# x transposed by VectorE in 32x32 squares instead of by TensorE, in a MoE feed-forward kernel

## The reference

```python
q_emb = relu(q @ W3 + b3)                           # cond: [128, 512]
v_sum = sum(v, axis=1, keepdims=True)               # over the 64 tokens of a sequence
h = relu(((n * v + v_sum) * q_emb[:, None, :]) @ W2 + b2)      # n = 64
scores = softmax(h @ gate_w.T)                      # 64 experts
topk_w, topk_i = top_k(scores, 6)
# first come, first served: each expert keeps 64 of the tokens that chose it
y = sum over kept choices of topk_w * (silu(h @ w_gate[e]) * (h @ w_up[e])) @ w_down[e]   # 512 -> 352 -> 512
shared = (silu(h @ sw_gate) * (h @ sw_up)) @ sw_down                                      # 512 -> 704 -> 512
out = x + y + shared
```

## Time and profile before

| | |
|---|---|
| median of 3 runs | 1278.72 us (1278.03 to 1279.66) |
| the profiled execution | 1280.25 us, of which the span of the profile is 1278.4 us |
| PE (TensorE) busy | 1254.0 us, 98% |
| DVE (VectorE) busy | 708.5 us, 55% |
| ACT (ScalarE) busy | 338.0 us, 26% |
| granted TensorE clock, mean | 0.995 of 2.4 GHz |
| one round of the first phase, 262.23 to 338.06 us | VectorE 62.3 us busy, ScalarE 26.5 |
| from 638.70 us, the second phase | VectorE 189 of 640 us busy, DMA engines 82% |

### The profile page before, as it was taken

How to read it: one execution, slowest core, us unless ns; L and a number is a source line. 1 busy time by engine, 2 the same in 40 slices (tenths; PEclk the granted TensorE clock), 3 DMA queues, 4 the chain that set the end, 5 groups by cost and what they waited for, 6 DMA issues and landing times.

```text
span 1278.4 us, 16131 instructions
## 1 busy us (share of the span) xinstructions
PE 1254.0 (98%) x6152; PEld 934.8 (73%) x6152; DVE 708.5 (55%) x1536; ACT 338.0 (26%) x550; POOL 144.1 (11%) x118
## 2 busy tenths in 40 slices
PE   5899999999999999999999999999999999999998
PEld 5687888888888888888867666666666666666666
DVE  6688888978888787886823233232232323323322
ACT  3444332332334333233212111121111201211110
POOL 0000000000000000000001222121222222212220
PEclk8899999999999999999999999999999999999999
DMA  7814417053441615325757989969979989898952
GB/s 199 254 38 134 138 48 220 9 177 91 128 144 38 194 41 182 91 86 132 280 196 278 284 266 294 318 236 283 326 220 330 308 246 291 283 300 267 294 127 77
DMA packets 129277, 250.92 MB, mean 196 GB/s; under 512 B 21296, under 2 KB 59312, under 8 KB 127024
## 3 DMA queue, kind: packets, MB, share of 16 engines
q1 hardware_dynamic: 117712, 224.71, 52.1%
q0 software_dynamic: 11488, 25.17, 9.8%
HBM read 197.14 MB, written 61.10 MB: 202 GB/s over the span
## 4 chain that ended last, share of the span: by engine, by line
PE 92%; DVE 3%; SPq 3%; DMA 1%; ACT 1%; issue 1%; ACTq 0%; DVEq 0%
PE bank L1213 22%; PE bank L1215 21%; PE bank L1214 21%; PE bank L1446 12%; PE bank L1469 7%; SPq L459 2%; PE bank L1230 2%; PE bank L1428 1%; PE bank L1336 1%; PE bank L1335 1%; PE bank L1271 1%; PE bank L1274 1%; PE bank L1455 1%; DMA hT<-h 1%; PE bank L1284 0%
## 5 line engine op out<-in xcount | busy, mean ns | idle before, releaser
L1213 PE MATMUL bank<-hh,gu 128*128 128x512 f32 x704 | 281.3, 400 | 0.1
L1215 PE MATMUL bank<-hh,gu 128*128 128x512 f32 x704 | 274.7, 390 | 0.0
L1214 PE MATMUL bank<-hl,gu 128*128 128x512 f32 x704 | 274.3, 390 | 0.0
L1213 PEld LDWEIGHTS bank<-hh,gu 128*128 128x128 f32 x704 | 132.5, 188 | 38.7 <-issue 12.8
L863 DVE TENSOR_TENSOR prod<-bank,prod 128x512 f32<-128x512 f32 x96 | 66.1, 689 | 165.8 <-PE bank L1215 144.0
L1215 PEld LDWEIGHTS bank<-hh,gu 128*128 128x128 f32 x704 | 132.1, 188 | 28.6
L1214 PEld LDWEIGHTS bank<-hl,gu 128*128 128x128 f32 x704 | 132.4, 188 | 25.3
L616 ACT ACTIVATE ah<-prod 128x512 fp32r<-128x512 f32 x96 | 60.6, 632 | 260.8 <-DVE prod L863 260.8
L1213 PE MATMUL bank<-sdh,ah 128*128 128x512 f32 x320 | 126.8, 396 | 0.0
L1214 PE MATMUL bank<-sdl,ah 128*128 128x512 f32 x320 | 124.6, 390 | 0.0
L1215 PE MATMUL bank<-sdh,al 128*128 128x512 f32 x320 | 124.6, 389 | 0.0
(11 more groups left out here) (117 smaller groups left out, 1604.9 us busy)
## 6 DMA issues: line engine op xcount, KB each, us to landing
wg<-in_L_ffn_w_gate_dram SPq DMA_DIRECT2D x64, 704.0 KB
wu<-in_L_ffn_w_up_dram SPq DMA_DIRECT2D x64, 704.0 KB
wd<-in_L_ffn_w_down_dram SPq DMA_DIRECT2D x64, 512.0 KB
table<-hrow SPq DMA_DIRECT2D x64, 256.0 KB, 4.3
x<-in_x_dram SPq DMA_DIRECT2D x15, 1024.0 KB, 8.4
wd<-in_L_ffn_w_down_dram SPq DMA_DIRECT2D x64, 192.0 KB
out_dram<-outst SPq DMA_DIRECT2D x36, 256.0 KB, 2.7
hT<-h SPq DMA_DIRECT2D x8, 1024.0 KB, 3.9
```

What stands on the lines that cost most here:

```text
L1213: nc.tensor.matmul(o, st_h, mv_h, start=first_mm, stop=False)
L1214: nc.tensor.matmul(o, st_h, mv_l, start=False, stop=False)
L1215: return nc.tensor.matmul(o, st_l, mv_h, start=False, stop=last_mm)
```

## The change

- TensorE no longer transposes x. SyncE loads x with 32 tokens by 128 features to a block, four DMAs a chunk (eight for chunk 0, in two halves), in pieces of 512 bytes. VectorE transposes each half chunk in 32x32 squares in place (`x_turn`), sums over 32 tokens (`x_sum`), adds the sums of two neighbouring blocks (`x_pair`), computes 64 x plus the sum (`x_shift`) and multiplies by q (`x_scale`), all in `x32` itself, 1024 elements a partition at a time. `split_xm` also goes by half chunks. Since features now stand on the partitions in another order, W2, W3, b3 and the gate weights are loaded or permuted to match; q is stored twice, once for each block of a sequence (`qb`).
- PSUM banks 3 and 4, free of x, go to the condition tiles.
- Chunk 1's condition tiles are made in halves, as chunk 0's, with `logits_raw(0)` between the halves; this is ahead of body 0 now. The order of loads changes: biases before x, no wait of SyncE for `hT` of chunk 0, which ScalarE's queue now stores, in quarters, right behind each tile.
- Routing: the low part of the logits is copied by ScalarE (`take_low`), the four sums of exponentials come with ScalarE's exponentials, and ScalarE copies the transposed ranks (`take_ranks`).
- VectorE's order in a body is new, with the two halves of a `merge` separated and laid between other work.

The diff, cut to its core:

```diff
-        xm = keep("xm", [P, 2, CH])
...
+        w3p = keep("w3p", [P, QC, D])
+        qb = keep("qb", [P, 2 * B, KC])
...
+        x32 = keep("x32", [P, 2, NB, P])
...
-            return bank[(5, 6, 1, 5)[oc] if n == 0 else 5 + oc % 2]
+            return bank[(5, 6, 1, 2)[oc] if n == 0 else (3, 4, 5, 6)[oc] if n == 1 else (4, 5, 6, 4)[oc]]
...
-                    sp.wait_ge(s.xt_filled, J * (n - 1))
-                if n == 0:
-                    for j in range(J):
-                        sp.dma_start(x32[:, 0, j, :], xf[j * P:(j + 1) * P, :]).then_inc(x_begun[j], 16)
-                else:
-                    sp.dma_start(x32[:, n % 2, :, :], xf[n * CH:(n + 1) * CH, :].rearrange(
-                        "(j p) d -> p j d", p=P)).then_inc(x_loaded[n % 2], 16)
+                    sp.wait_ge(s.xml_ready, 2 * (n - 1))
+                for half in ((0, 1) if n == 0 else (None,)):
+                    b = slice(0, NB) if half is None else slice(half * (NB // 2), (half + 1) * (NB // 2))
+                    rows = xf[n * CH + b.start * SQ:n * CH + b.stop * SQ, :].rearrange("(b i) d -> i b d", i=SQ)
+                    for q in range(P // SQ):
+                        sp.dma_start(x32[q * SQ:(q + 1) * SQ, n % 2, b, :], rows[:, :, q * P:(q + 1) * P]).then_inc(
+                            x_loaded[n % 2] if half is None else x_begun[half], 16)
...
             def store_hT(u):
-                sp.wait_ge(s.cond_taken, KC * (2 * u + 1))
-                sp.dma_start(hT[u], h32[:, :, :].rearrange("p k t -> p (k t)")).then_inc(s.hT_stored, 16)
+                for k in range(KC):
+                    sp.wait_ge(s.cond_taken, KC * 2 * u + k + 1)
+                    sp.dma_start(hT[u][:, k * CH:(k + 1) * CH], h32[:, k, :]).then_inc(hT_stored[k], 16)
...
+            with nc.allow_non_contiguous_dma(reason="two vectors of 512 elements, once"):
+                sp.dma_start(conds[:, :], cond).then_inc(s.cond_loaded, 16)
+                sp.dma_start(w3s[:, :, :], W3.rearrange("(k p) o -> p k o", p=P)).then_inc(s.w3_loaded, 16)
+                for q in range(P // SQ):
+                    for b, c in ((b3, b3c), (b2, b2c)):
+                        sp.dma_start(c[q * SQ:(q + 1) * SQ, :],
+                                     b[q * P:(q + 1) * P].rearrange("(k j) -> j k", j=SQ)).then_inc(s.bias_loaded, 16)
             load_x(0)
...
             load_x(2)
-            store_hT(0)
...
+            def take_low(n):
+                act.wait_ge(s.logits_filled, n + 1)
+                wait(act, s.z_ready, n)
+                parts = logits_bank(n)[:, :].rearrange("p (j h e) -> p h j e", j=J, h=2)
+                copy(lg[:, :, :], parts[:, 1, :, :]).then_inc(s.llow_ready, 1)
+            def take_ranks(i):
+                act.wait_ge(s.ranksT_filled, i + 1)
+                wait(act, s.merge_step, MERGE_STEPS * i)
+                copy(cand[:, CAP:CAP + CH], bank[7][:, :]).then_inc(s.cand_ready, 1)
...
-                nc.scalar.activation(ez[:, :, :], z[:, :, :], ACT.Exp).then_inc(s.exp_ready, 1)
+                for j in range(J):
+                    op = nc.scalar.activation(ez[:, j, :], z[:, j, :], ACT.Exp, accum_out=ssum[:, j:j + 1])
+                op.then_inc(s.exp_ready, 1)
...
-            take_cond(0, 0)
-            take_cond(0, 1)
+            def first_cond(oc):
+                take_cond(0, oc)
+                act.dma_start(hT[0][:, oc * CH:(oc + 1) * CH], h32[:, oc, :]).then_inc(hT_stored[oc], 16)
+            first_cond(0)
+            first_cond(1)
             split_xm(1, 0)
+            first_cond(2)
+            first_cond(3)
+            split_piece(1)
             split_xm(1, 1)
-            take_cond(0, 2)
-            split_xm(1, 2)
-            split_xm(1, 3)
-            take_cond(0, 3)
-            split_piece(1)
             split_piece(2)
             take_lraw(0)
...
-                    elif oc == 0:
+                    if i > 0 and oc == 0:
+                        take_low(a)
+                    if i > 0 and oc == 2:
                         exp_scores(a)
...
+                if 0 < i < ND - 1:
                     split_xm(c, 0)
                 silu(v, 0)
-                if more:
-                    split_xm(c, 1)
+                if i > 0:
+                    take_low(b)
...
+            def x_flat(n, half):
+                return x32[:, n % 2, half * (NB // 2):(half + 1) * (NB // 2), :].rearrange("p b (k i) -> p (b k) i", i=SQ)
+            def spread(t):
+                return t.rearrange("p b k -> p (b k)").unsqueeze(2).to_broadcast([P, KC * NB // 2, SQ])
+            def x_turn(n, half):
+                if n == 0:
+                    dve.wait_ge(x_begun[half], 64)
+                elif half == 0:
+                    dve.wait_ge(x_loaded[n % 2], 64 * (n // 2 + n % 2))
+                flat = x32[:, n % 2, half * (NB // 2):(half + 1) * (NB // 2), :].rearrange("p b c -> p (b c)")
+                nc.vector.transpose(flat, flat).then_inc(x_step[half], 1)
+            def x_sum(n, half):
+                dve.wait_ge(x_step[half], 4 * n + 1)
+                nc.vector.reduce_sum(xpart[:, half, :, :], half_of(n, half), AX).then_inc(x_step[half], 1)
+            def x_pair(n, half):
+                dve.wait_ge(x_step[half], 4 * n + 2)
+                pairs = xpart[:, half, :, :].rearrange("p (b t) k -> p b t k", t=2)
+                nc.vector.tensor_tensor(vsum[:, half, :, :].rearrange("p (b t) k -> p b t k", t=2),
+                                        pairs[:, :, 0:1, :].to_broadcast([P, NB // 4, 2, KC]),
+                                        pairs[:, :, 1:2, :].to_broadcast([P, NB // 4, 2, KC]),
+                                        ALU.add).then_inc(x_step[half], 1)
+            def x_shift(n, half):
+                x = x_flat(n, half)
+                dve.wait_ge(x_step[half], 4 * n + 3)
+                nc.vector.scalar_tensor_tensor(x, x, float(N), spread(vsum[:, half, :, :]), ALU.mult,
+                                               ALU.add).then_inc(x_step[half], 1)
+            def x_scale(n, half):
+                x = x_flat(n, half)
+                first_block = n * NB + half * (NB // 2)
+                dve.wait_ge(x_step[half], 4 * n + 4)
+                if n == 0:
+                    dve.wait_ge(s.q_ready, 1)
+                nc.vector.tensor_tensor(x, x, spread(qb[:, first_block:first_block + NB // 2, :]),
+                                        ALU.mult).then_inc(s.xm_ready, 1)
...
+            def split_xm(n, half):
+                dve.wait_ge(s.xmh_ready, 2 * n + half + 1)
                 high, low = split_x(n)
-                lower(xm_tile(low, j), xm_place(n, j).rearrange("p (k t) -> p k t", k=KC),
-                      xm_tile(high, j)).then_inc(s.xml_ready, 1)
...
+                    x_turn(c, 0)
+                    take_rows(b, 0)
+                    x_sum(c, 0)
+                    take_rows(b, 1)
+                    x_pair(c, 0)
+                    take_rows(b, 2)
+                    x_shift(c, 0)
+                    take_rows(b, 3)
+                    x_scale(c, 0)
+                    take_down(v - 1, 3)
+                    if i == 1:
+                        merges(0, (2, 3))
+                    if i == 2:
+                        merge(1, 6)
+                    m = [(0, 6), (0, 7)] + [(1, r) for r in range(6)] if i == 1 else [(i, r) for r in range(NR)]
+                    route(b)
                     product(v, 0)
-                    route(a)
+                    split_xm(c, 0)
                     split_a(v, 0)
+                    if i == 1:
+                        merge(0, 4)
+                    if i == 2:
+                        merge(1, 7)
+                    x_turn(c, 1)
                     product(v, 1)
-                    split_xm(c, 0)
-                    split_xm(c, 1)
+                    x_sum(c, 1)
                     split_a(v, 1)
...
+                    x_pair(c, 1)
+                    x_shift(c, 1)
                     product(v, 2)
                     if i == 1:
...
+                        merge(0, 5)
+                    x_scale(c, 1)
                     split_a(v, 2)
...
+                    merge_top(*m[0])
+                    x_turn(d, 0)
+                    merge_drop(*m[0])
+                    split_xm(c, 1)
                     product(v, 3)
...
+            x_half(0, 0)
+            x_turn(0, 1)
             split_xm(0, 0)
+            split_piece(0, slice(0, 2))
+            x_sum(0, 1)
+            split_piece(0, slice(2, 4))
+            x_pair(0, 1)
+            x_shift(0, 1)
+            x_scale(0, 1)
+            x_turn(1, 0)
             split_xm(0, 1)
-            split_piece(0, slice(0, 2))
-            scale_xt(0, 2, 4)
-            split_piece(0, slice(2, 4))
-            split_xm(0, 2)
-            split_xm(0, 3)
-            take_xt(1, 0)
+            x_sum(1, 0)
+            x_pair(1, 0)
+            x_shift(1, 0)
+            x_turn(1, 1)
+            x_scale(1, 0)
```

(63 more changed lines are left out.)

457 lines of the change are left out of this document (208 added, 249 removed).

## The result

The changed kernel takes 1282.8 us (median of 8 runs, 1279.2 to 1284.8) against 1279.5 us for the kernel before (8 runs beside it): a ratio of 1.0026, 95% interval 1.0015 to 1.0037. The forecast was 31 us faster with 0.94 on faster; it came out 0.26% slower, outside the range of 1241 to 1261.

What follows compares the result with a forecast made beforehand. TensorE was taken as the bound, busy for all of a 75.83 us round. Savings of 21.1 + 2.6 + 1.8 + 8.0 less 2.8 given back made 30.7 us, so 1278.72 became 1248.0 us; range 1241 to 1261.

Steps and rivals of the forecast that it cites:

- Transfers: Loads of x in 512-byte pieces, four DMAs a chunk: chunk c lands by 281, needed at 285.2, so no cost.
- that cover: Chunk c of x landing by 281, before VectorE needs it at 285.2; without it, each us late costs one per round.
- The pair of transposes: x transposes leaving TensorE: 0.88 us a pair, 24 pairs in bodies 1 to 6, 21.1 us saved.
- VectorE's durations: 1024-element operations on x: 1210 ns each, 1.14 us when overlapped; VectorE's work about 63.2 us a round.
- The opening: Before body 0: earlier start and no wait for hT's store; gate/up starts at 51.5, gain 8.0 us, bounds 3 and 10.
- The second phase: From 638.7 on: same instructions and TensorE load, so zero change.
- The give-back at `product(v, 0)`: TensorE waits at the fifth gate/up tile: 0.3 us a round in bodies 1 to 6, 1.0 more in body 1; 2.8 us.
- slack of 0.1 us: At the fifth gate/up tile: `product(v, 0)` ready at 299.9, TensorE wants it at 300.1; stated margin 0.1 us.
- The first rival: VectorE's chain becomes the bound at `product(v, 0)`; 12 us come back, giving 1260 us; chance 0.20.
- exponentials with sums: ScalarE's four in `exp_scores(a)`, ahead of `take_cond(b, 3)`: about 0.8 us, at most twice that; 1.6 to 1.9 causes lateness.
- Body 0: the step on `h`: Condition tile now ahead of the exponentials removes TensorE's 1.8 us wait for `h`; three transpose pairs save another 2.6 us.
- the fourth rival: Waits of about 4 us for `product(v, 0)` lower TensorE's clock in bodies 1 to 6: 40 us, 1288; chance 0.04.

Runs made afterwards that it cites:

- second experiment: The changed kernel with the load of the next chunk c issued just ahead of the DRAM-to-DRAM copy of x instead of behind it: 1257.2 us, ratio 0.983.
- The sixth experiment: The changed kernel with chunk c's load right behind the score store, plus a new VectorE and ScalarE order, mainly in the first pair of chunks: 1245.6 us, ratio 0.974.
- the first experiment: The changed kernel with the load of the next body's chunk c issued right behind the store of chunk b's scores: 1252.3 us, ratio 0.979.

## Why the prediction was wrong, step by step

**The step that failed: Transfers.** It took the issue time of chunk c from the trace of before, 272.36, added a landing of under 9 us, found it in place by 281 and charged nothing. Two terms of it were wrong, and each has its number now; the third, the need, was right.
- *The queue ahead of the load.* `load_x(c)` stands behind `store_rows(c)`, `store_out` and `keep_x(c)` in SyncE's queue, and `store_rows(c)` waits for the fourth `take_rows(c, ...)`. The change spreads these between merges on VectorE, and counted from `logits_raw(c)` they end 7.0 us later (10.9 instead of 3.8) and the load is issued 6.4 us later (16.7 instead of 10.3). The prediction followed the queue forwards (what gains issues, what is next behind them), not backwards to what the load itself waits for. Putting the rows back gives 23 us back.
- *The landing.* It used the median of one 256 KB load and of one 1 MB load. The last of four pieces behind a copy of 1 MB needs 10.9 to 11.7 us; without that copy 8.4 to 9.2; as one DMA behind it 8.6 to 10.8.
- *The need.* Before, x was wanted by the transposes on TensorE; now it is wanted at the point where VectorE has finished `split_h(b, 3)`, 283.8 in the trace of after. This the prediction had (285.2 on its time base).

With the true terms, counted from `logits_raw(c)` at 260.63: issued at 16.7, landed 11.5 later at 28.2, needed at 23.2 (283.80), hence 5.0 late, for which TensorE waits 3.3 and pays 1.8 at the lower clock: 5.1 in this round. The queue is the term that decides: with the old issue and the true landing x is there at 21.8 (10.3 + 11.5), in time; with the new issue and the prediction's landing of 8.6 it is there at 25.3, 2.1 late. The prediction itself said that "if that cover went, each us too late would be a us per round" and gave this no chance of its own; it should have been a rival: some 5 us in each of six rounds is the whole sum of 30.7.

**What was right.** The pair of transposes at 0.88 us: 75.83 - 72.30 = 3.53 = 4 x 0.88 in the rounds from the third pair on. VectorE's durations, groups by shape of the changed kernel:

```profile
L834 DVE STREAM_TRANSPOSE x<-x 128x1024 f32<-128x1024 f32 x32 | 39.5, 1236 | 32.4 <-DMA x<-in_x_dram 32.4
L851 DVE SCALAR_TENSOR_TENSOR x<-x,vsum 128x1024 f32<-128x1024 f32 x32 | 38.8, 1214 | 0.6
...
L860 DVE TENSOR_TENSOR x<-x,qb 128x1024 f32<-128x1024 f32 x32 | 38.6, 1208 | 0.1
L838 DVE TENSOR_REDUCE xpart<-x 128x32 f32<-128x1024 f32 x32 | 38.5, 1202 | 0.1
```

They are within 3% of the 1210 ns of the earlier trace rows, and VectorE's work in a round is 62.7 us where 63.2 was forecast. The opening: `logits_raw(1)` 8.0 us earlier, and gate/up's first matmul at 51.59 where 51.5 was forecast. The second phase: zero.

**The give-back at `product(v, 0)` (0.3 us in each of six rounds and 1.0 more in body 1)** was too much for five rounds and too little for body 1: with x in time the slack of 0.1 us held in the later rounds (72.30, no wait), and body 1's round takes 75.33, 3.0 more, 1.0 of it waits for products, 1.28 the wait for chunk d's `xml` and 0.8 what such waits cost besides their length. The first rival is refuted as a bound in itself, though its slack of 0.1 us is real (second experiment). The exponentials with sums take 0.97 us for four, nearer to the forecast's lower figure of 0.8 than to the upper.

**Body 0: the step on `h` failed.** 2.6 + 1.8 us were forecast, 0.9 came. The wait for `h` is still there, 1.64 us at 93.88 instead of 1.84: `take_cond(c, 0)` now precedes the exponentials, but not `split_a(v, 5)`, which waits for `product(v, 5)`, and that stands on VectorE behind the split of a 128x1536 weight piece (1.75 us) and `route(b)`. New waits came with it: 0.83 for a `silu` behind the exponentials' two table loads, and 0.53, with another 1.25 in body 1, that the list puts down to "issue" and that end when VectorE's `xml` is done. The sixth experiment confirms these readings together; its edits weren't run one by one, so the share of each is not shown.

**The clock (the fourth rival).** The mechanism came, its place was another: the wait is for `outst`, behind the load, not for `product(v, 0)`. The waits of 4.50, 3.85, 3.30 and 2.25 us (the last at 525.22) in the changed kernel were each followed by matmuls 0.43 us apart. Those of 2.22 us (at 372.89) and 1.88 (at 448.86) were not, and the window from 338.04 to 414.35 has clock 1.00. So the length of the wait alone does not decide: 2.25 and 2.22 us came out differently, and with x in one DMA a wait of 1.97 us was followed by the lower clock and one of 1.89 us (at 215.67) was not:

```profile
516.85 0.50 PE L1317 MATMUL bank<-hh,gu 128*128 128x512 f32 x1 [1.97 <-DVE outst L920]
...
518.31 0.63 PE L1319 MATMUL bank<-hh,gu 128*128 128x512 f32 x1
518.74 0.63 PE L1317 MATMUL bank<-hh,gu 128*128 128x512 f32 x1
```

What else decides is not shown here. The Trainium skill ("TensorE: Matmul & The Clock Gate", section HAM oscillation) tells of a kernel that fell back at each of its waits for data, which were some 3 to 5 us long. The trace agrees for its own waits of 3.30 us and more, and shows the same fall behind shorter ones.

**The sum with x in time.** 21.1 + 2.6 + 1.8 + 8.0 - 2.8 = 30.7 was forecast; the span of the first experiment is 28.3 under that of before (1278.4 - 1250.1). By the marks of both traces: the opening 0.8 better than forecast (`logits_raw(1)` at 48.77), body 0 3.5 worse, body 1 1.3 worse, the five later rounds 1.5 better: -2.5, which is the 2.4 missing up to rounding. In medians, the result lies 34.8 us above the forecast (1282.8 - 1248.0); 30.5 of that is the late load (1282.8 - 1252.3), and 4.3 the rest; 0.8 of the rest is that the kernel before took 1279.5 and not 1278.7 us in the runs beside it.

## What to carry to other kernels

When a change makes an engine want a transfer earlier, take the issue time not from the old trace but from the new program: go back through the queue that issues it, and through what each wait in that queue stands behind on its own engine. A load that depends on nothing new belongs ahead of stores that wait for fresh results, and ahead of bulk copies that nobody is waiting for. And where a stall grows to some 2 us or more, count the slower clock that can follow it; here the four rounds with such a fall lost 7.3 of 29.6 us to it.

## What the runs showed of the hardware

- A 1 MB copy from DRAM to DRAM, issued just ahead on the same queue, delayed the landing of four 256 KB loads from 8.4 to 9.2 us to 10.9 to 11.7 us. The median landing of a piece, over the loads of both chunks of a pair, went from 5.5 to 7.0 us.
- An exponential with a sum is two entries on ScalarE. Of the timeline of the changed kernel:

```profile
280.27 0.24 ACT L655 ACTIVATE ez<-z 128x64 f32<-128x64 f32 x1
280.41 0.19 ACT L655 ACTIVATION_READ_ACCUMULATOR ez<-z 128x1 f32 x1
280.50 0.24 ACT L655 ACTIVATE ez<-z 128x64 f32<-128x64 f32 x1
```

  Four of them are 0.24 us apart, 0.97 in all, against 0.417 for the one exponential of 256 elements.
- A short wait costs TensorE 0.2 to 0.3 us beyond its length, at a granted clock of 1.00: three waits in body 0 of the first experiment cost 0.84 us (48.41 - 47.57), two in the round from 338.04 of the changed kernel 0.44 (72.74 - 72.30).
- A wait of about 2 us can be followed by some 3 us at the lower clock or not (2.25 and 1.97 us were, 2.22 and 1.89 us were not); the four rounds of the changed kernel in which it was had 1.8 to 1.9 us more of TensorE work.
